# Two attention layers on one core: every attention taken key block by key block, and the side work of the next unit moved behind it

## The chip, the cores and the metric

The kernel runs on one core of a Trainium2 chip. The metric is the device time of one execution in microseconds (us), the median of several. A core has a matrix engine (TensorE, "PE" in the profile; PEld is its weight loads), VectorE (DVE), ScalarE (ACT), GpSimd (POOL) and SyncE (SP), which run their own instruction streams and wait for each other by semaphores.

## The reference

Two layers in sequence on x of 2 images, 32 x 32 pixels, 256 channels (1024 positions an image). Each layer is a group norm, an attention of one head over all positions, and a residual:

```
def layer(x, gamma, beta, wq, bq, wk, bk, wv, bv, wp, bp):      # eps 1e-5, then 1e-6
    xn = group_norm(x, gamma, beta)        # 32 groups of 8 channels, over all positions
    q, k, v = conv1x1(xn, wq, bq), conv1x1(xn, wk, bk), conv1x1(xn, wv, bv)   # B, 1024, 256
    scores = einsum('bnc,bmc->bnm', q, k) / sqrt(256)
    attn = softmax(scores, axis=-1)
    return conv1x1(einsum('bnm,bmc->bnc', attn, v), wp, bp) + x
```

## The kernel before

**Units and chunks.** A unit u is one image in one layer; four units run one after the other (image 0 and 1 in layer 0, then in layer 1). Each has two chunks of 512 queries (c = 2u and 2u + 1), each chunk four query blocks j of 128 and eight key blocks kb of 128. In the loop over units, `before` is the last chunk of the unit before, `first` and `second` are the two of this unit.

**Folded weights.** wq and wk are multiplied once (A), so are wv and wp (Wx). A unit has: t = A by the normalised rows xn (`t_product`, half h = 0 or 1 for the two chunks, two tiles k each), value blocks (`values`, 8), score tiles S (keys by queries, `scores(c, kb)`, 8 a chunk), attention (`attend(c, j, kb)`). Every operand is split into two parts, hi and lo, and each product is three matmuls (hi by lo, lo by hi, hi by hi), to keep the accuracy.

**The path of a score tile.** PE writes it to a PSUM bank; ACT copies it to S (`score_copy`); DVE takes the running maximum into R from the bank (`running_max`), which frees the bank. When all eight are in, PE turns R round (`maxima_by_query`), DVE reduces it (`query_shift`), PE spreads the result over X (`shift_to_all`), DVE adds it to each tile of S (`shifted`), ACT takes the exponential twice (`exponentials`: P_hi, and S in full), POOL subtracts them (`p_low`: P_lo). Then PE can attend. A query block's output is divided by its sum, and added to x in xnat, by DVE (`output`: a reciprocal and a scalar_tensor_tensor), which frees its bank.

**Banks.** Six PSUM banks form a ring. `ring_order` is the list of all tiles (t, V, S, O) in the order in which PE writes them; each waits until the tile six places earlier has been read (`wait_for_bank`). X and Z are the other two banks; Z takes the transposed rows of x and the small products of the group norm.

**The next unit's norm** runs beside this unit's attention: PE transposes pairs of row blocks r = 0 to 3 into Z (`next_rows`), ACT copies them to xraw (`raw_rows`), DVE takes bn_stats (`statistics_of`), after the fourth the aggregate mv (`channel_statistics`), PE multiplies it by group_mean (`mean_of_groups`), DVE forms var_c in four small instructions (`group_deviation`), PE averages it (`variance_of_groups`), DVE and POOL make gain and shift (`variance`, `power`, `affine_map`), then `normalise`, `xn_high`, `xn_low`, and `t_product(u + 1, 0, k)`.

**Order.** Each engine's stream is written out by hand, and each engine does its instructions strictly in that order. PE in a unit: values, scores(first), attention(before), scores(second), attention(first). Before the change the six inner chunks attend query block by query block (all eight key blocks of j = 0, then j = 1, ...), the first and the last chunk key block by key block. The small PE steps stand between query blocks:

```
for j in range(QB):
    ...
    if j == 0: maxima_by_query(following)
    if j == 1: shift_to_all(following); before_third()   # t_product(u, 1, k) in attention(before)
    if j == 2: before_last()                             # next_rows(u+1, 2), or t_product(u+1, 0, k)
```

Of the kernel before, what the change touches and what calls it, by code (L numbers as in the profile page):

```python
# [19 lines left out]
def two_attention_layers(nc, x, layers, vectors, out):  # L20
# [15 lines left out]
    KC = C // P  # L36
    NB = N // P
    HALVES = N // BANK
    CHUNKS = UNITS * HALVES
    QB = BANK // P  # L40
# [26 lines left out]
    for u in range(1, UNITS):  # L67
        ring_order += [("V", u, m) for m in range(NB)]
        ring_order += [("S", 2 * u, kb) for kb in range(NB)]
        ring_order += [("O", 2 * u - 1, j) for j in range(2)]  # L70
        ring_order += [("t", u, 1, k) for k in range(KC)]
        ring_order += [("O", 2 * u - 1, j) for j in range(2, QB)]
        ring_order += [("S", 2 * u + 1, kb) for kb in range(NB)]
        if u < UNITS - 1:
            ring_order += [("O", 2 * u, j) for j in range(3)]
            ring_order += [("t", u + 1, 0, k) for k in range(KC)]
            ring_order += [("O", 2 * u, j) for j in range(3, QB)]
        else:
            ring_order += [("O", 2 * u, j) for j in range(QB)]
    ring_order += [("O", CHUNKS - 1, j) for j in range(QB)]  # L80
    ring_place = {tile: n for n, tile in enumerate(ring_order)}

    with ExitStack() as ctx:
# [66 lines left out]
        Z = ps("Z")  # L150
# [160 lines left out]
        def _(act):  # L311
# [117 lines left out]
            for u in range(1, UNITS):  # L429
# [14 lines left out]

                t_high(u, 1, 0)
                exponentials(first, 0)
                t_high(u, 1, 1)
                exponentials(first, 1)
                exponentials(first, 2)
                if more:  # L450
                    raw_rows(u + 1, 2, Z)
                exponentials(first, 3)

                for kb in range(NB):
                    score_copy(second, kb)
                    if kb == 0 and more:
                        raw_rows(u + 1, 3, Z)
                    if kb in (0, 1, 2, 4):
                        exponentials(first, {0: 4, 1: 5, 2: 6, 4: 7}[kb])

                if more:
                    for q in range(TQ):
                        xn_high(u + 1, q)
                for kb in range(3):
                    exponentials(second, kb)
                if more:
                    for k in range(KC):
                        t_high(u + 1, 0, k)
                exponentials(second, 3)
            for kb in range(4, NB):  # L470
# [4 lines left out]
        def _(dve):  # L475
# [217 lines left out]
            for u in range(1, UNITS):  # L693
# [12 lines left out]

                output(before, 0)
                query_shift(first)
                output(before, 1)
                shifted(first, 0)  # L710
                t_low(u, 1, 0)
                shifted(first, 1)
                t_low(u, 1, 1)
                shifted(first, 2)
                shifted(first, 3)
                output(before, 2)
                shifted(first, 4)
                if more:
                    statistics_of(u + 1, 2)
                shifted(first, 5)  # L720
                output(before, 3)
                shifted(first, 6)

                for kb in range(1, NB):
                    running_max(second, kb)
                    if kb == 1:
                        shifted(first, 7)
                        if more:
                            statistics_of(u + 1, 3)
                            channel_statistics(u + 1)  # L730
                    if more and kb == 5:
                        group_deviation(u + 1)
                    if more and kb == 7:
                        variance(u + 1)
                if more:
                    affine_map(u + 1)

                output(first, 0)
                query_shift(second)
                if more:  # L740
                    normalise(u + 1)
                    xn_low(u + 1, 0)
                    xn_low(u + 1, 1)
                output(first, 1)
                shifted(second, 0)
                shifted(second, 1)
                if more:
                    xn_low(u + 1, 2)
                    xn_low(u + 1, 3)
                output(first, 2)  # L750
                shifted(second, 2)
                if more:
                    t_low(u + 1, 0, 0)
                shifted(second, 3)
                if more:
                    t_low(u + 1, 0, 1)
                output(first, 3)
                shifted(second, 4)
                shifted(second, 5)
# [7 lines left out]
        def _(pe):  # L767
# [191 lines left out]

            def attention(c, following, before_third, before_last):  # L960

                pe.wait_ge(po_P, (c + 1) * NB)
                for j in range(QB):
                    wait_for_bank("O", c, j)
                    for kb in range(NB):
                        attend(c, j, kb)
                    if j == 0:
                        maxima_by_query(following)
                    if j == 1:
                        shift_to_all(following)  # L970
                        before_third()
                    if j == 2:
                        before_last()

            def attention_by_keys(c, kb):
# [23 lines left out]
            for kb in range(NB):  # L999
                scores(1, kb)  # L1000
            for kb in range(NB):
                attention_by_keys(0, kb)
                if kb == 1:
                    maxima_by_query(1)
                if kb == 3:
                    shift_to_all(1)
            for k in range(KC):
                t_product(1, 0, k)

            for u in range(1, UNITS):  # L1010
                before, first, second = 2 * u - 1, 2 * u, 2 * u + 1
                more = u < UNITS - 1

                def second_half():
                    for k in range(KC):
                        t_product(u, 1, k)

                def third_rows():
                    if more:
                        next_rows(u + 1, 2)  # L1020

                def next_first_half():
                    if more:
                        for k in range(KC):
                            t_product(u + 1, 0, k)

                for m in range(NB):
                    values(u, m)

                for kb in range(NB):  # L1030
                    scores(first, kb)
                    if more and kb in (2, 5):
                        next_rows(u + 1, kb // 3)

                attention(before, first, second_half, third_rows)

                for kb in range(NB):
                    scores(second, kb)
                    if kb == 0 and more:
                        next_rows(u + 1, 3)  # L1040
                    if more and kb == 4:
                        mean_of_groups(u + 1)
                    if more and kb == 6:
                        variance_of_groups(u + 1)

                attention(first, second, lambda: None, next_first_half)

            for kb in range(NB):
                attention_by_keys(CHUNKS - 1, kb)

# [31 lines left out]
```

## Time and profile before

| | |
|---|---|
| median of 3 timed runs | 272.69 us (272.2 to 272.89) |
| the profiled execution's own time | 271.55 us |
| its span (first to last instruction) | 269.6 us |
| PE busy | 257.4 us, 95% of the span |
| DVE, ACT, POOL busy | 172.5, 151.1, 110.5 us |
| granted clock of PE, the loop over units | full (1.00) |
| second score stage of unit 1, PE | 109.55 to 122.32 us |

The timeline rows give start and length in us, the engine, the line of the kernel, the operation with its tiles, and in brackets the idle time before it with what ended it. A PE row's length is longer than the distance to the next one, since matmuls overlap; for PE the distances between starts are what counts.

### The profile page before, as it was taken

The page shows a single profiled execution, that of the slowest core. Times are in us where ns is not written, and L with a number is a line of the kernel's source. Part 1 is how long each engine was busy: PE and PEld are TensorE (multiplying, and loading weights), DVE is VectorE, ACT ScalarE, POOL GpSimd, SP SyncE. Part 2 cuts the span into 40 slices and gives each one's busy share as a digit, 9 for nine tenths or more (in the row PEclk, how much of TensorE's full clock was granted, in tenths as well). Part 3 has the DMA queues.
Part 4 walks back from the last instruction along what each step waited for, and adds up shares of the span by engine and source line. Part 5 has one row for each costly group of instructions (what it writes and reads, how often), then busy time and mean ns, then how long its engine had stood idle before and what let it go on. Part 6 is the DMA issues. An engine that isn't in the chain of part 4 may idle for free.

```text
span 269.6 us, 4591 instructions
## 1 busy us (share of the span) xinstructions
PE 257.4 (95%) x1650; PEld 232.8 (86%) x1650; DVE 172.5 (64%) x436; ACT 151.1 (56%) x295; POOL 110.5 (41%) x111
## 2 busy tenths in 40 slices
PE   3899899999999999999999999999999999999994
PEld 2788689889988899879998899879998899889993
DVE  0599576786687557475977557475977547454613
ACT  3465454499778507670687606680577507670750
POOL 2015300187345914451255813461065724550680
PEclk9999999999999999999999999999999999999999
DMA  5960000000000000000000000000110000100102
GB/s 136 368 239 1 0 1 0 2 0 2 0 1 0 4 2 0 0 1 2 0 1 2 0 2 0 0 0 2 40 41 0 4 19 19 39 2 19 58 3 78
DMA packets 5965, 7.37 MB, mean 27 GB/s; under 512 B 556, under 2 KB 4664, under 8 KB 5944
## 3 DMA queue, kind: packets, MB, share of 16 engines
q1 hardware_dynamic: 5920, 7.08, 7.8%
q8 instruction: 13, 0.21, 0.4%
q14 instruction: 8, 0.07, 0.1%
q10 hardware_dynamic: 24, 0.01, 0.0%
HBM read 4.99 MB, written 2.10 MB: 26 GB/s over the span
## 4 chain that ended last, share of the span: by engine, by line
PE 75%; DVE 8%; ACT 8%; issue 6%; DMA 1%; POOL 1%; DVEq 0%; ACTq 0%; POOLq 0%
PE ring L953 10%; PE ring L955 10%; PE ring L954 10%; PE ring L914 9%; PE ring L916 9%; PE ring L915 9%; PE ring L900 3%; PE ring L901 3%; PE ring L902 3%; ACT S L401 2%; PE Z L812 2%; ACT P_hi L400 2%; PE ring L887 2%; PE ring L888 2%; PE ring L889 2%
## 5 line engine op out<-in xcount | busy, mean ns | idle before, releaser
L286 POOL TENSOR_TENSOR P_lo<-S,P_hi 128x512 fp32r<-128x512 f32 x64 | 82.9, 1302 | 104.3 <-ACT S L401 104.3
L953 PE MATMUL ring<-V,P_hi 128*128 128x258 f32 x256 | 73.6, 287 | 0.0
L955 PE MATMUL ring<-V,P_lo 128*128 128x258 f32 x256 | 72.4, 283 | 0.0
L954 PE MATMUL ring<-V,P_hi 128*128 128x256 f32 x256 | 72.3, 282 | 0.0
L393 ACT COPY S<-ring 128x512 f32<-128x512 f32 x64 | 37.6, 587 | 37.4 <-PE ring L916 34.6
L914 PE MATMUL ring<-t_hi,xn_lo 128*128 128x512 f32 x128 | 51.4, 402 | 0.8 <-DVE t_lo L607 0.8
L400 ACT ACTIVATE P_hi<-S 128x512 fp32r<-128x512 f32 x64 | 40.7, 635 | 19.3 <-DVE S L642 17.7
L916 PE MATMUL ring<-t_hi,xn_hi 128*128 128x512 f32 x128 | 50.1, 391 | 0.0
L915 PE MATMUL ring<-t_lo,xn_hi 128*128 128x512 f32 x128 | 49.9, 390 | 0.0
L954 PEld LDWEIGHTS ring<-V,P_hi 128*128 128x128 f32 x256 | 48.5, 189 | 0.5
L953 PEld LDWEIGHTS ring<-V,P_hi 128*128 128x128 f32 x256 | 48.4, 189 | 0.5
L625 DVE TENSOR_TENSOR R<-ring,R 128x512 f32<-128x512 f32 x48 | 33.0, 687 | 24.7 <-ACT S L393 24.1
L955 PEld LDWEIGHTS ring<-V,P_lo 128*128 128x128 f32 x256 | 48.5, 190 | 0.0
L642 DVE TENSOR_TENSOR S<-X,S 128x512 f32<-128x512 f32 x64 | 42.2, 680 | 0.0
L401 ACT ACTIVATE S<-S 128x512 f32<-128x512 f32 x64 | 39.9, 624 | 0.0
L914 PEld LDWEIGHTS ring<-t_hi,xn_lo 128*128 128x128 f32 x128 | 24.1, 188 | 5.5 <-DVE t_lo L607 1.2
L916 PEld LDWEIGHTS ring<-t_hi,xn_hi 128*128 128x128 f32 x128 | 24.0, 188 | 5.2
L915 PEld LDWEIGHTS ring<-t_lo,xn_hi 128*128 128x128 f32 x128 | 24.1, 188 | 4.3
L281 POOL TENSOR_TENSOR xnat<-xnat,out_bias 128x256 f32<-128x256 f32 x32 | 23.0, 754 | 6.3 <-DVE out_bias L517 6.3
L379 ACT ACTIVATE t_hi<-ring,att 128x512 fp32r<-128x512 f32 x16 | 10.6, 681 | 25.0 <-PE ring L889 25.0
L648 DVE RECIPROCAL row_inv<-ring 128x1 f32<-128x1 f32 x32 | 5.2, 164 | 24.0 <-PE ring L955 24.0
L900 PE MATMUL ring<-Wx_hi,xn_lo 128*128 128x258 f32 x64 | 18.5, 290 | 0.2 <-DVE xnat L652 0.2
(100 smaller groups left out, 350.3 us busy)
## 6 DMA issues: line engine op xcount, KB each, us to landing
xnat<-in_x SPq DMA_DIRECT2D x8, 256.0 KB, 6.7
out<-xnat SPq DMA_DIRECT2D x16, 128.0 KB, 1.9
wide<-in_vectors SPq DMA_DIRECT2D x2, 384.0 KB, 6.9
w_wq<-in_L_conv_wq SPq DMA_DIRECT2D x2, 256.0 KB, 4.8
w_wk<-in_L_conv_wk SPq DMA_DIRECT2D x2, 256.0 KB, 4.9
w_wv<-in_L_conv_wv SPq DMA_DIRECT2D x2, 256.0 KB, 6.5
w_wp<-in_L_conv_wp SPq DMA_DIRECT2D x1, 256.0 KB, 6.5
w_wp<-in_L_conv_wo SPq DMA_DIRECT2D x1, 256.0 KB, 6.8
```

The source lines that it names most:

```text
L286: nc.gpsimd.tensor_tensor(P_lo[:, tile, :], S[:, tile, :], P_hi[:, tile, :].bitcast(F32), ALU.subtract).then_inc(po_P, 1)
L393: nc.scalar.copy(S[:, tile_of(c, kb), :], bank_of("S", c, kb)[:]).then_inc(ac_S, 1)
L400: nc.scalar.activation(P_hi[:, tile, :], S[:, tile, :], ACT.Exp)
L401: nc.scalar.activation(S[:, tile, :], S[:, tile, :], ACT.Exp).then_inc(ac_P, 1)
L625: nc.vector.tensor_tensor(R[:], bank_of("S", c, kb)[:], earlier, ALU.max).then_inc(dv_R, 1)
L642: nc.vector.tensor_tensor(tile, X[:], tile, ALU.add).then_inc(dv_D, 1)
L914: nc.tensor.matmul(bank[:], xn_lo[:, kc, keys], t_hi[:, kc, cols], start=(kc == 0), stop=False)
L915: nc.tensor.matmul(bank[:], xn_hi[:, kc, keys], t_lo[:, kc, cols], start=False, stop=False)
L916: last = nc.tensor.matmul(bank[:], xn_hi[:, kc, keys], t_hi[:, kc, cols], start=False, stop=(kc == KC - 1))
L953: nc.tensor.matmul(bank[:, 0:C + 2], P_hi[:, tile, mine], v[:, kb, 0:C + 2], start=(kb == 0), stop=False)
L954: nc.tensor.matmul(bank[:, 0:C], P_hi[:, tile, mine], v[:, kb, C + 2:VX], start=False, stop=False)
L955: last = nc.tensor.matmul(bank[:, 0:C + 2], P_lo[:, tile, mine], v[:, kb, 0:C + 2], start=False, stop=(kb == NB - 1))
```

## The change

1. All eight chunks attend key block by key block: for each kb the four query blocks in turn, so four banks are open until the last kb; a chunk's waits on P_lo are one for each kb. The small steps stand behind key blocks 1 (maxima), 3 (shift) and, in attention(before), 5 (t of this unit's second half).
2. t of the next unit's first half stands behind attention(first), no longer ahead of its last query block; `ring_order` follows.
3. Rows 2 and 3 of the next unit are transposed behind score blocks 1 and 3 of `second` (before: in attention(before), and behind block 0); the mean of the groups is behind block 5 (4), the variance behind block 7 (6).
4. ACT and DVE are rewritten to match: the copies of rows 2 and 3 behind the copies of score blocks 2 and 4, their statistics behind running maxima 3 and 4; t_high behind four exponentials; the four outputs of a chunk together at its end.

```diff
@@ -67,16 +67,12 @@
     for u in range(1, UNITS):
         ring_order += [("V", u, m) for m in range(NB)]
         ring_order += [("S", 2 * u, kb) for kb in range(NB)]
-        ring_order += [("O", 2 * u - 1, j) for j in range(2)]
+        ring_order += [("O", 2 * u - 1, j) for j in range(QB)]
         ring_order += [("t", u, 1, k) for k in range(KC)]
-        ring_order += [("O", 2 * u - 1, j) for j in range(2, QB)]
         ring_order += [("S", 2 * u + 1, kb) for kb in range(NB)]
+        ring_order += [("O", 2 * u, j) for j in range(QB)]
         if u < UNITS - 1:
-            ring_order += [("O", 2 * u, j) for j in range(3)]
             ring_order += [("t", u + 1, 0, k) for k in range(KC)]
-            ring_order += [("O", 2 * u, j) for j in range(3, QB)]
-        else:
-            ring_order += [("O", 2 * u, j) for j in range(QB)]
     ring_order += [("O", CHUNKS - 1, j) for j in range(QB)]
     ring_place = {tile: n for n, tile in enumerate(ring_order)}
@@ -442,31 +438,26 @@
                     if more and kb in (3, 6):
                         raw_rows(u + 1, kb // 3 - 1, Z)
 
-                t_high(u, 1, 0)
-                exponentials(first, 0)
-                t_high(u, 1, 1)
-                exponentials(first, 1)
-                exponentials(first, 2)
-                if more:
-                    raw_rows(u + 1, 2, Z)
-                exponentials(first, 3)
+                for kb in range(4):
+                    exponentials(first, kb)
+                for k in range(KC):
+                    t_high(u, 1, k)
 
                 for kb in range(NB):
                     score_copy(second, kb)
-                    if kb == 0 and more:
-                        raw_rows(u + 1, 3, Z)
-                    if kb in (0, 1, 2, 4):
-                        exponentials(first, {0: 4, 1: 5, 2: 6, 4: 7}[kb])
+                    if kb in (0, 1, 3, 5):
+                        exponentials(first, {0: 4, 1: 5, 3: 6, 5: 7}[kb])
+                    if more and kb in (2, 4):
+                        raw_rows(u + 1, 1 + kb // 2, Z)
 
                 if more:
                     for q in range(TQ):
                         xn_high(u + 1, q)
-                for kb in range(3):
+                for kb in range(4):
                     exponentials(second, kb)
                 if more:
                     for k in range(KC):
                         t_high(u + 1, 0, k)
-                exponentials(second, 3)
             for kb in range(4, NB):
                 exponentials(CHUNKS - 1, kb)
 
@@ -704,58 +695,44 @@
                     if more and kb in (3, 6):
                         statistics_of(u + 1, kb // 3 - 1)
 
-                output(before, 0)
                 query_shift(first)
-                output(before, 1)
-                shifted(first, 0)
-                t_low(u, 1, 0)
-                shifted(first, 1)
-                t_low(u, 1, 1)
-                shifted(first, 2)
-                shifted(first, 3)
-                output(before, 2)
-                shifted(first, 4)
-                if more:
-                    statistics_of(u + 1, 2)
+                for kb in range(5):
+                    shifted(first, kb)
+                for k in range(KC):
+                    t_low(u, 1, k)
+                for j in range(QB):
+                    output(before, j)
                 shifted(first, 5)
-                output(before, 3)
-                shifted(first, 6)
 
                 for kb in range(1, NB):
                     running_max(second, kb)
-                    if kb == 1:
-                        shifted(first, 7)
-                        if more:
-                            statistics_of(u + 1, 3)
-                            channel_statistics(u + 1)
-                    if more and kb == 5:
+                    if kb < 3:
+                        shifted(first, kb + 5)
+                    if more and kb in (3, 4):
+                        statistics_of(u + 1, kb - 1)
+                    if more and kb == 4:
+                        channel_statistics(u + 1)
+                    if more and kb == 6:
                         group_deviation(u + 1)
-                    if more and kb == 7:
-                        variance(u + 1)
                 if more:
+                    variance(u + 1)
                     affine_map(u + 1)
-
-                output(first, 0)
                 query_shift(second)
                 if more:
                     normalise(u + 1)
                     xn_low(u + 1, 0)
                     xn_low(u + 1, 1)
-                output(first, 1)
                 shifted(second, 0)
                 shifted(second, 1)
                 if more:
                     xn_low(u + 1, 2)
                     xn_low(u + 1, 3)
-                output(first, 2)
-                shifted(second, 2)
-                if more:
-                    t_low(u + 1, 0, 0)
-                shifted(second, 3)
-                if more:
-                    t_low(u + 1, 0, 1)
-                output(first, 3)
-                shifted(second, 4)
+                for kb in range(2, 5):
+                    shifted(second, kb)
+                for j in range(QB):
+                    output(first, j)
+                    if more and j in (1, 3):
+                        t_low(u + 1, 0, j // 2)
                 shifted(second, 5)
-            def attention(c, following, before_third, before_last):
-
-                pe.wait_ge(po_P, (c + 1) * NB)
-                for j in range(QB):
-                    wait_for_bank("O", c, j)
-                    for kb in range(NB):
-                        attend(c, j, kb)
-                    if j == 0:
-                        maxima_by_query(following)
-                    if j == 1:
-                        shift_to_all(following)
-                        before_third()
-                    if j == 2:
-                        before_last()
-
...
@@ -998,12 +960,18 @@
                     shift_to_all(0)
             for kb in range(NB):
                 scores(1, kb)
-            for kb in range(NB):
-                attention_by_keys(0, kb)
-                if kb == 1:
-                    maxima_by_query(1)
-                if kb == 3:
-                    shift_to_all(1)
+            def attention(c, behind_sixth):
+
+                for kb in range(NB):
+                    attention_by_keys(c, kb)
+                    if c < CHUNKS - 1 and kb == 1:
+                        maxima_by_query(c + 1)
+                    if c < CHUNKS - 1 and kb == 3:
+                        shift_to_all(c + 1)
+                    if kb == 5:
+                        behind_sixth()
+
+            attention(0, lambda: None)
             for k in range(KC):
                 t_product(1, 0, k)
 
@@ -1014,15 +982,6 @@
                 def second_half():
                     for k in range(KC):
                         t_product(u, 1, k)
-
-                def third_rows():
-                    if more:
-                        next_rows(u + 1, 2)
-
-                def next_first_half():
-                    if more:
-                        for k in range(KC):
-                            t_product(u + 1, 0, k)
 
                 for m in range(NB):
                     values(u, m)
@@ -1032,21 +991,23 @@
                     if more and kb in (2, 5):
                         next_rows(u + 1, kb // 3)
 
-                attention(before, first, second_half, third_rows)
+                attention(before, second_half)
 
                 for kb in range(NB):
                     scores(second, kb)
-                    if kb == 0 and more:
-                        next_rows(u + 1, 3)
-                    if more and kb == 4:
+                    if more and kb in (1, 3):
+                        next_rows(u + 1, 2 + kb // 2)
+                    if more and kb == 5:
                         mean_of_groups(u + 1)
-                    if more and kb == 6:
+                    if more and kb == 7:
                         variance_of_groups(u + 1)
 
-                attention(first, second, lambda: None, next_first_half)
-
-            for kb in range(NB):
-                attention_by_keys(CHUNKS - 1, kb)
+                attention(first, lambda: None)
+                if more:
+                    for k in range(KC):
+                        t_product(u + 1, 0, k)
+
+            attention(CHUNKS - 1, lambda: None)
 
 
 # ---- launch: one core; inputs and outputs as the reference has them ----
```

The three places that matter, as the instruction streams have them. In PE's stream, in the second score stage of unit 1, the mean of the groups (`Z<-mv,group_mean`) before, between score block 4 (ring0) and 5 (ring1):

```order
L916 MATMUL ring0<-t_hi,xn_hi 128x512
L914 MATMUL ring0<-t_hi,xn_lo 128x512
L915 MATMUL ring0<-t_lo,xn_hi 128x512
L916 MATMUL ring0<-t_hi,xn_hi 128x512
L819 MATMUL Z<-mv,group_mean 128x2
L914 MATMUL ring1<-t_hi,xn_lo 128x512
```

And now, between block 5 (ring1) and 6 (ring2):

```order
L893 MATMUL ring1<-t_hi,xn_hi 128x512
L891 MATMUL ring1<-t_hi,xn_lo 128x512
L892 MATMUL ring1<-t_lo,xn_hi 128x512
L893 MATMUL ring1<-t_hi,xn_hi 128x512
L796 MATMUL Z<-mv,group_mean 128x2
L891 MATMUL ring2<-t_hi,xn_lo 128x512
```

It moved back by one score block (the lines' numbers differ since the file is shorter). DVE's stream in the same stage before, from the last two `shifted` to the variance's input (R are running maxima, BN_STATS the statistics of rows 3, BN_AGGR makes mv):

```order
L625 TENSOR_TENSOR R<-ring,S 128x512 [waits ac_S]
L642 TENSOR_TENSOR S<-X,S 128x512 [waits pe_M]
L489 BN_STATS bn<-xraw 128x6 [waits ac_xT]
L489 BN_STATS bn<-xraw 128x6
L523 BN_AGGR mv<-bn 128x2 [waits dv_bn]
L523 BN_AGGR mv<-bn 128x2
L625 TENSOR_TENSOR R<-ring,R 128x512 [waits dv_R,ac_S] x4
L529 COPY gmean<-Z 128x2 [waits pe_gm]
```

And now:

```order
L616 TENSOR_TENSOR R<-ring,R 128x512 [waits dv_R,ac_S]
L480 BN_STATS bn<-xraw 128x6 [waits ac_xT]
L480 BN_STATS bn<-xraw 128x6
L616 TENSOR_TENSOR R<-ring,R 128x512 [waits dv_R,ac_S]
L480 BN_STATS bn<-xraw 128x6 [waits ac_xT]
L480 BN_STATS bn<-xraw 128x6
L514 BN_AGGR mv<-bn 128x2 [waits dv_bn]
L514 BN_AGGR mv<-bn 128x2
L616 TENSOR_TENSOR R<-ring,R 128x512 [waits dv_R,ac_S] x2
L520 COPY gmean<-Z 128x2 [waits pe_gm]
```

The aggregation stood behind the first running maximum of the stage (block 1); it stands behind the fourth (block 4), and two maxima instead of four lie between it and the deviation. ACT's stream in that stage before, from the copy of score block 0 (L393) on; L318 is the copy of rows 3:

```order
L393 COPY S<-ring 128x512 [waits pe_S,po_P]
L318 COPY xraw<-Z 128x2x256 [waits dv_xl,pe_xT]
L400 ACTIVATE P_hi<-S 128x512 [waits dv_D,pe_O]
L401 ACTIVATE S<-S 128x512
L393 COPY S<-ring 128x512 [waits pe_S,po_P]
```

And now, from the copy of block 2 (L389) on; the first L314 is rows 2, the second rows 3:

```order
L389 COPY S<-ring 128x512 [waits pe_S,po_P]
L314 COPY xraw<-Z 128x2x256 [waits dv_xl,pe_xT]
L389 COPY S<-ring 128x512 [waits pe_S,po_P]
L396 ACTIVATE P_hi<-S 128x512 [waits dv_D,pe_O]
L397 ACTIVATE S<-S 128x512
L389 COPY S<-ring 128x512 [waits pe_S,po_P]
L314 COPY xraw<-Z 128x2x256 [waits dv_xl,pe_xT]
```

The copy of rows 3 moved from behind block 0 to behind block 4.

## Rows read from the trace of the kernel before

**Rows 1.** The page: span, busy times, granted clock in 40 slices.
```profile
span 269.6 us, 4591 instructions
...
PE 257.4 (95%) x1650; PEld 232.8 (86%) x1650; DVE 172.5 (64%) x436; ACT 151.1 (56%) x295; POOL 110.5 (41%) x111
...
PEclk9999999999999999999999999999999999999999
```

**Rows 2.** Waits of PE: in total, times, longest; two of the six rows.
```profile
PE Z L823 <- DVE var_c L535: 1.2, 2, 0.6
...
PE ring L900 <- DVE xnat L652: 0.2, 1, 0.2
```

**Rows 3.** Timeline of PE, second score stage of unit 1.
```profile
110.94 0.60 PE L812 MATMUL Z<-ident,xnat 128*128 128x128 f32 x4
111.30 0.48 PE L914 MATMUL ring<-t_hi,xn_lo 128*128 128x512 f32 x1
...
116.86 0.28 PE L819 MATMUL Z<-mv,group_mean 128*128 128x2 f32 x2
...
120.61 0.38 PE L823 MATMUL Z<-var_c,group_mean 128*128 128x2 f32 x2 [0.62 <-DVE var_c L535]
```

**Rows 4.** Timeline of ACT, the same stage.
```profile
111.20 0.59 ACT L393 COPY S<-ring 128x512 f32<-128x512 f32 x1 [2.57 <-PE ring L916]
111.68 0.59 ACT L318 COPY xraw<-Z 128x512 f32<-128x512 f32 x1
...
113.21 0.58 ACT L393 COPY S<-ring 128x512 f32<-128x512 f32 x1
```

**Rows 5.** Timeline of DVE, the same stage.
```profile
113.83 0.69 DVE L625 TENSOR_TENSOR R<-ring,S 128x512 f32<-128x512 f32 x1 [2.72 <-ACT S L393]
114.44 0.68 DVE L642 TENSOR_TENSOR S<-X,S 128x512 f32<-128x512 f32 x1
115.03 0.74 DVE L489 BATCH_NORM_STATS2 bn<-xraw 128x6 f32<-128x256 f32 x2
115.81 0.39 DVE L523 BATCH_NORM_AGGREGATE mv<-bn 128x2 f32<-128x24 f32 x2
...
119.34 0.69 DVE L625 TENSOR_TENSOR R<-ring,R 128x512 f32<-128x512 f32 x1 [0.92 <-ACT S L393]
...
120.39 0.16 DVE L535 TENSOR_TENSOR var_c<-dev,mv 128x2 f32<-128x2 f32 x1
```

**Rows 6.** Timeline of PE, attention by keys (60), by queries (215); 24 matmuls between.
```profile
60.60 0.29 PE L953 MATMUL ring<-V,P_hi 128*128 128x258 f32 x1
...
63.51 0.60 PE L940 MATMUL X<-ident,R 128*128 128x128 f32 x4
...
215.43 0.29 PE L953 MATMUL ring<-V,P_hi 128*128 128x258 f32 x1
...
218.31 0.60 PE L940 MATMUL X<-ident,R 128*128 128x128 f32 x4
```

**Rows 7.** Timeline of PE and DVE, end of a query block and its output.
```profile
96.84 0.60 PE L940 MATMUL X<-ident,R 128*128 128x128 f32 x4
...
97.31 0.48 DVE L652 SCALAR_TENSOR_TENSOR xnat<-ring,row_inv,xnat 128x256 f32<-128x256 f32 x1
```

**Rows 8.** Timeline of PE, ACT and DVE, from unit 0 to unit 1.
```profile
74.39 0.39 PE L887 MATMUL ring<-xn_hi,A_lo 128*128 128x512 f32 x1
...
77.56 0.39 PE L900 MATMUL ring<-Wx_hi,xn_lo 128*128 128x258 f32 x1 [0.16 <-DVE xnat L652]
...
75.39 1.30 ACT L379 ACTIVATE t_hi<-ring,att 128x512 fp32r<-128x512 f32 x2
...
76.08 0.75 DVE L607 SCALAR_TENSOR_TENSOR t_lo<-ring,att,t_hi 128x512 fp32r<-128x512 f32 x1 [0.89 <-ACT t_hi L379]
...
77.02 0.48 DVE L652 SCALAR_TENSOR_TENSOR xnat<-ring,row_inv,xnat 128x256 f32<-128x256 f32 x1
...
77.68 0.48 DVE L652 SCALAR_TENSOR_TENSOR xnat<-ring,row_inv,xnat 128x256 f32<-128x256 f32 x1
```

## The prediction, made before the changed kernel was run

> **What bounds the kernel now.** I read the page first: TensorE (PE) is busy 95% of a span of 269.6 us, at the full granted clock in nearly every slice [rows 1]. Then the waits of PE: inside the loop over units it waits for the variance of the groups, twice, 1.2 us in all, and once 0.2 us for an output row [rows 2]; the list's other four rows name two transfers, t_lo and neg_shift, and stand in unit 0 or ahead of it. So from the first unit on the time is the number of matmuls times their pace. A change of order can win about those waits and no more; each new wait of PE is added in full, since nothing later has slack to give it back. The question is therefore which of PE's semaphores will come after PE gets there.
>
> All times below are starts of PE instructions ("PE reaches"), because a PE row's length overlaps the next row. By that measure one key block of scores costs 1.36 us: rows of x end at 111.30 and the mean of the groups is reached at 116.86, that is 5.56 us for four key blocks, of which 0.11 us is the first matmul behind a transposition (0.34 us to its follower against 0.23 us) [rows 3].
>
> **The change part by part.**
>
> *Key block by key block.* Every matmul stays. The weights of each matmul change as they did, the outputs go over four banks in turn, and each key block has a wait of its own on P_lo instead of one wait for all eight. The first and the last chunk run so already: 24 matmuls of attention took 2.91 us there (60.60 to 63.51) and 2.88 us query by query (215.43 to 218.31) [rows 6]. The difference is 0.03 us in 24, at most 0.7 us for the six chunks that change; two rows that close don't separate it from nothing, so the sum takes 0 and the range 0.7. Could it gain? Only if PE waited for P_lo at the start of a chunk; none of the six rows of PE's waits is for P_lo [rows 2], so the looser wait gives nothing. The Trainium skill, "TensorE: Matmul & The Clock Gate", section "A second HAM failure mode: psum-queue depth-cycling", speaks against such an order: cycling through PSUM banks made short idle times between groups of matmuls, and the clock fell again and again. By the row the order costs 0, by the page it could cost much; the trace of this case doesn't agree with it.
>
> *Rows 2 and 3 of x and their statistics, two tiles later.* This is the term that decides. Before, rows 2 were transposed inside the attention and rows 3 behind score block 0 of the second chunk, and PE asked for the mean of the groups behind block 4. The aggregates were ready at 115.81 + 0.39 = 116.20 us [rows 5], PE came at 116.86 [rows 3]: 0.66 us to spare. Now rows 2 stand behind block 1, rows 3 behind block 3, ScalarE (ACT) copies rows 3 only behind its copy of score block 4, and VectorE (DVE) takes their statistics behind the running maximum of block 4. PE asks for the mean behind block 5. The chain, from the moment PE ends block 4:
> - ACT starts copying the block 0.26 us later (110.94 to 111.20) [rows 3, 4].
> - DVE starts the running maximum 0.62 us after the copy starts (113.21 to 113.83), and the next instruction 0.61 us later [rows 4, 5]. That is 1.49 us. The copy of rows 3 ends at 0.26 + 0.48 + 0.59 = 1.33 us [rows 4], so it isn't last.
> - Two bn_stats and the gap to the aggregation 0.78 us, the aggregation 0.39 us [rows 5], the semaphore 0.06 us (var_c ends at 120.55, PE goes on at 120.61) [rows 3, 5].
> The sum is 2.72 us. PE has one block of 1.36 us in that time and then stands: **1.36 us of a new wait**, for the mean, in each of the two units that have a successor: +2.7 us. Nothing before it on ACT is late: two exponentials take 1.05 us (111.68 + 0.48 to 113.21) [rows 4], so block 3 with its exponentials ends 0.26 + 0.48 + 1.05 = 1.79 us after PE's end of block 3, and block 4's copy isn't due before 1.36 + 0.45 (transpositions and refill, rows 3) + 0.26 = 2.07 us. Queued behind the waiting matmul are the score blocks 6 and 7; the whole PE stream moves.
>
> *The variance wait.* Before: behind block 6, waiting for var_c, which came at 120.55 after a running maximum started at 119.34, 1.21 us [rows 5]. PE's idle time there is 0.62 us by the row [rows 3]; from start to start it is 0.26 + 0.62 + 1.21 + 0.06 - 1.36 = 0.79 us, and the difference is the tail of the last matmul. After: behind block 7, var_c behind the maximum of block 6: the same lag of one block, so the same 0.79 us. The exponentials that now stand before that copy end 1.79 us after block 5, and the new wait gives them time. This term is 0: the old wait stays and the new one comes on top.
>
> *Outputs at the end of an attention, four at once.* Behind attention(before), three times, score block 0 of the second chunk needs the bank of that attention's first output. PE ends a query block's last matmul, and the output row is written 0.95 us later (96.84 to 97.31 + 0.48) [rows 7]; the first of four queries ends 9 matmuls of 0.12 us, 1.09 us, before PE is through. So the bank is free 0.14 us before it is wanted, less 0.06 us for the semaphore. I take no stall, but a lost early load of weights, the 0.11 us of a refill, three times: +0.3 us. The next outputs follow at 0.66 us (77.02 to 77.68) [rows 8] and the score blocks at 1.36 us. DVE must be free: t_lo of the second half now comes just before. PE's t ends 24 matmuls, 2.9 us, ahead of the end; 0.26 us and t_hi of 0.65 us and t_lo of 0.75 us [rows 8] end at 1.2 us ahead. The first output's reciprocal is due 0.27 us before its row of 97.31, that is 0.2 us behind its last matmul and 0.9 us ahead of the end: 0.3 us of slack for DVE. Thin, but there. If it is missed by as much as one t_lo, 0.75 us, three times, that is +2.2 us: the upper end of this term.
>
> *t of the next unit behind the attention.* Unit 1 has this order already, and pays for it: value block 2 waits 0.16 us for its bank, held by an output that queued behind t_lo on DVE [rows 8]. There ACT came to t_hi late (75.39, when PE's first t tile had ended at 74.39) because of exponentials. In the changed units the fourth exponential ends, by the same lengths, over a microsecond before t_hi is due, so t_lo starts 0.26 + 0.69 us behind the first t tile (six matmuls at 0.23 us, 1.4 us), 2.35 us after the attention; the third output row is written at 2.35 + 0.94 + 0.48 = 3.8 us [rows 8], and the bank is wanted behind both t tiles and two value blocks of six matmuls at 0.12 us, at 2.8 + 2 x 0.72 = 4.2 us. I take 0; the bound is the row of unit 1, 0.4 us from start to start, twice: 0.8 us.
>
> *Sum.* 2.7 + 0 + 0 + 0.3 + 0 = +3.0 us. The profiled execution took 271.55 us around its span, so 274.6 us; it lies 1.1 us below the median of the timed runs, 272.69, from which the same sum gives **275.7 us**, 1.1% slower.
>
> **Rivals.**
> - *The mean's wait doesn't come.* For it: it is reckoned, not seen. Against: for that the statistics would have to land 1.36 us sooner, and every link above is a row of this kernel. Then only the 0.3 us is left: 273.0 us, no change that can be told (a measurement of this kernel tells about 0.3%, 0.8 us). 0.11.
> - *More waits than one.* DVE is late with the first output, or value blocks wait as in unit 1: 2.2 + 0.8 us at the outside, about half of it likely if at all: 277.2 us. For it: the slack is 0.1 to 0.3 us. 0.13.
> - *Faster.* The variance wait goes because DVE, freed of outputs in that stretch, has var_c 0.79 us sooner, and the mean isn't late. Both would win 2 x 0.79: 271.1 us. It decides at var_c 0.79 us after block 6's maximum instead of 1.21 us behind it, which four dependent instructions don't allow. 0.05.
> - *The clock falls.* In the trace it held through PE's idle 0.62 us [rows 1, 3]; the new idle is 1.2 us by the same measure, which no row inside the loop shows. If PE ran at 1.2 GHz for the rest of that stage, two score blocks, 2.7 us more per unit: 281 us. The Trainium skill, "TensorE: Matmul & The Clock Gate", section "HAM oscillation — how this bites in real kernels", has the clock fall in idle gaps; its example waits longer than this. 0.02. That it falls through the order by keys itself, every 24 matmuls then taking 2.9 us more, 24 times, +70 us, has [rows 6] against it: under 0.01.
>
> **How the numbers follow.** The forecast has 0.68. Its own range is 274.7 to 276.7. The whole range, 273.2 to 277.8 us, takes in half of the first rival's ground and most of the second. Faster by over 0.3% is the third rival, 0.05; within 0.3% is the first with a little of the forecast's low side, 0.13; slower 0.82.
>
> **What the changed profile would show.** Among PE's waits a new row: group_mean for DVE's mv (the aggregation), two times, 1.1 to 1.3 us each by the row's idle time; the variance row still two times 0.6 us. The second score stage of units 1 and 2 longer by 1.4 us, unit 3 as long as before. 24 matmuls of attention in 2.9 us. Score block 0 of the second chunk with a small wait or none for xnat. The prediction is wrong if PE lists no wait for mv, or if a wait for xnat or t_lo stands above it.

## The result and the profile after

The changed kernel takes 275.15 us (median of 4 runs, 274.87 to 275.88), the kernel before 272.44 us (4 runs, 271.52 to 272.89): ratio 1.0108, 95% interval 1.0073 to 1.0142. That is 1.1% slower, 2.7 us, against a forecast of 275.7 us, +3.0.

The waits of PE in the changed kernel (in total, times, longest) answer to [rows 2]:

```profile
PE Z L796 <- DVE mv L514: 2.5, 2, 1.2
...
PE Z L800 <- DVE var_c L526: 1.5, 2, 0.9
...
PE ring L877 <- DVE xnat L643: 0.2, 1, 0.2
```

The first row is new: PE waits at the mean of the groups (L796) for the aggregation of the statistics, once in each of the two units that have a successor. The variance row, 1.2 us before, is still there and grew by 0.3 us. No row names P_lo. The xnat row is that of unit 1's start, as before.

Busy time by unit, before and then after (stretches from the first value block of units 1, 2 and 3; the last ends with PE's last matmul; behind the length stand the busy times of PE, PEld, DVE, ACT and POOL, then the granted clock):

```profile
75.79:137.52 61.73, 60.95 (x397) 55.24 (x396) 41.68 (x103) 34.93 (x68) 27.12 (x26) 1.00 0.01 1
137.52:198.73 61.21, 60.59 (x399) 55.15 (x397) 41.11 (x102) 34.94 (x68) 26.96 (x26) 1.00 0.03 8
198.73:265.63 66.90, 66.90 (x462) 62.33 (x460) 36.68 (x83) 34.78 (x68) 32.74 (x30) 1.00 0.06 18
```

```profile
76.42:140.12 63.70, 61.41 (x398) 55.08 (x396) 42.12 (x103) 35.80 (x69) 28.38 (x27) 1.00 0.00 1
140.12:203.09 62.97, 61.13 (x397) 54.98 (x396) 41.17 (x102) 35.53 (x68) 26.77 (x25) 1.00 0.02 5
203.09:270.08 66.99, 66.99 (x461) 62.40 (x459) 35.82 (x83) 34.60 (x67) 31.07 (x28) 1.00 0.06 20
```

The first number behind the stretch is its length. Units 1 and 2 are 1.97 and 1.76 us longer, unit 3 by 0.09 us: 3.82 us in this pair of profiles, nearly all of it where side work for a next unit exists. The clock is full in all six stretches. The interval of the ratio is 2.0 to 3.9 us, so the profiles' 3.82 us lie at its upper end.

Where the two measures differ, the setup is part of it: unit 1 starts at 75.79 before and at 76.42 after, and in the profiles of the changed kernel's variants below, whose code up to there is the same, anywhere from 75.27 to 76.49. The units repeat more closely: one of these variants (e8) changes nothing but waits for P_lo, on which PE doesn't stand in units 1 and 2, and has them within 0.03 us of the changed kernel's. So the sums below use the units' lengths; but each is from one profiled execution, and the timed runs are given beside them.

### The profile page after: what moved, and what is told of

It is laid out like the page before. It is cut to its first block, busy times and chain, and to the rows that moved or that the text cites. A ratio compares the mean times of both kernels' runs of the same rounds, so it can differ in the third digit from the quotient of the medians.

```text
span 274.1 us, 4591 instructions
## 1 busy us (share of the span) xinstructions
PE 259.1 (95%) x1650; PEld 233.0 (85%) x1650; DVE 172.2 (63%) x436; ACT 152.4 (56%) x295; POOL 109.9 (40%) x111
## 4 chain that ended last, share of the span: by engine, by line
PE 75%; DVE 9%; ACT 7%; issue 6%; DMA 1%; POOL 1%; DVEq 0%; ACTq 0%; POOLq 0%
PE ring L930 10%; PE ring L932 10%; PE ring L931 10%; PE ring L891 9%; PE ring L893 9%; PE ring L892 9%; PE ring L877 3%; PE ring L878 2%; PE ring L879 2%; ACT S L397 2%; ACT S L389 2%; PE Z L789 2%; PE ring L865 2%; PE ring L864 2%; PE ring L866 2%
## 5 line engine op out<-in xcount | busy, mean ns | idle before, releaser
L389 ACT COPY S<-ring 128x512 f32<-128x512 f32 x64 | 37.5, 586 | 41.1 <-PE ring L893 37.0
L633 DVE TENSOR_TENSOR S<-X,S 128x512 f32<-128x512 f32 x64 | 41.4, 682 | 8.6 <-PE X L923 8.6
L598 DVE SCALAR_TENSOR_TENSOR t_lo<-ring,att,t_hi 128x512 fp32r<-128x512 f32 x16 | 11.6, 746 | 11.5 <-ACT t_hi L375 11.5
L878 PE MATMUL ring<-Wx_lo,xn_hi 128*128 128x258 f32 x64 | 18.2, 284 | 0.0
```

Source lines behind the costliest of these rows:

```text
L389: nc.scalar.copy(S[:, tile_of(c, kb), :], bank_of("S", c, kb)[:]).then_inc(ac_S, 1)
L633: nc.vector.tensor_tensor(tile, X[:], tile, ALU.add).then_inc(dv_D, 1)
```

## The chain behind the new wait, row by row

The changed kernel's timelines of PE, ACT and DVE, unit 1, second score stage; score block 4 ends at 117.73, where block 5's first matmul starts:

```profile
117.73 0.40 PE L891 MATMUL ring<-t_hi,xn_lo 128*128 128x512 f32 x1
...
118.88 0.39 PE L893 MATMUL ring<-t_hi,xn_hi 128*128 128x512 f32 x1
120.52 0.35 PE L796 MATMUL Z<-mv,group_mean 128*128 128x2 f32 x2 [1.25 <-DVE mv L514]
...
124.62 0.38 PE L800 MATMUL Z<-var_c,group_mean 128*128 128x2 f32 x2 [0.88 <-DVE var_c L526]
...
117.98 0.59 ACT L389 COPY S<-ring 128x512 f32<-128x512 f32 x1 [0.26 <-PE ring L893]
118.46 0.59 ACT L314 COPY xraw<-Z 128x512 f32<-128x512 f32 x1
...
118.60 0.69 DVE L616 TENSOR_TENSOR R<-ring,R 128x512 f32<-128x512 f32 x1 [0.55 <-ACT S L389]
119.21 0.74 DVE L480 BATCH_NORM_STATS2 bn<-xraw 128x6 f32<-128x256 f32 x2
119.98 0.39 DVE L514 BATCH_NORM_AGGREGATE mv<-bn 128x2 f32<-128x24 f32 x2
```

From PE's end of block 4 the copy starts 0.25 us later, the maximum 0.62 us behind it, the statistics 0.61 us behind that, the aggregation 0.77 us on, and ends at 120.37; PE goes on at 120.52. That is 2.79 us, reckoned 2.72: from the aggregation's end to PE it took 0.15 us, not 0.06. The last matmul of block 5 starts at 118.88, and its follower could have at 119.11, so PE stood 1.41 us from start to start, 1.25 us by the row. Reckoned: 1.36.

## Experiments

"Loop" is the length of units 1 to 3 in the profile, as above: 189.84 us before, 193.66 us after. Each ratio is to runs of the kernel before that were taken beside the experiment: 23 of them with median 272.12 us for e1 to e4, 19 with median 271.71 us for e5 to e8.

**The mean one block later** (label e1_mean_later):

```diff
-                    if more and kb == 5:
+                    if more and kb == 6:
                         mean_of_groups(u + 1)
```

> The changed kernel with one number altered: PE asks for the mean of the groups behind score block 6 instead of 5. Theory (the whole loss is PE waiting for the aggregation of the statistics, 1.4 us in each of two units): the aggregation lands 2.8 us after block 4 ends, PE now comes 2.7 us after it, so the wait for mv shrinks to 0 to 0.1 us, the wait for var_c stays at 0.6 to 0.9 us, and the time falls by 2.6 to 2.8 us, to the time of the kernel before or 0.3 us above it. Rival (order by keys or bunched outputs cost): it stays 1 us or more above the kernel before.

Measured: 272.50 us, ratio to the kernel before 1.0004 (0.9982 to 1.0026); loop 190.37 us. PE's waits no longer name mv, and for var_c, where the expectation had 0.6 to 0.9 us each, are down to

```profile
PE Z L800 <- DVE var_c L526: 0.9, 2, 0.5
```

One number gives back 3.29 us of the loop's 3.82: 2.8 us are the two waits, 0.5 us more is saved at the variance, where the mean's own two matmuls and the refill behind them (0.22 + 0.11 us) now stand between block 6 and PE's arrival. The order by keys with everything else of the change is left 0.53 us above the kernel before in the loop, and can't be told from it by the timed runs. That isn't yet the price of the rest, since the wait for var_c is 0.3 us shorter here than in the kernel before; e6 and e7 compare the two orders with neither wait.

**The mean one block earlier** (e2_mean_earlier; the same edit with 4):

> The changed kernel with PE asking for the mean behind score block 4 instead of 5. Theory: PE's wait for mv grows by the one score block it no longer has, 1.36 us a unit, to 2.6 us of idle time by the row, and the time by 2.7 us, to about 278 us. Rival (other instructions behind the wait absorb it): less than 1.5 us more.

Measured: 280.79 us, 5.6 us above the changed kernel where 2.7 was expected, ratio 1.0318 (1.0266 to 1.0371). The four timed runs spread from 279.04 us, with a mean granted clock of 0.993, to 282.78 us, with 0.982. The profiled execution is the slowest of them: its loop is 200.6 us, 6.9 us above the changed kernel's. The wait grew as the theory says, from 1.25 to 2.63 us by the row. Most of the rest is the clock. Timeline of PE in unit 2, and the stretches around the two waits (length, busy times, then the granted clock):

```profile
183.45 0.40 PE L893 MATMUL ring<-t_hi,xn_hi 128*128 128x512 f32 x1
186.47 0.56 PE L796 MATMUL Z<-mv,group_mean 128*128 128x2 f32 x2 [2.63 <-DVE mv L514]
186.89 0.78 PE L891 MATMUL ring<-t_hi,xn_lo 128*128 128x512 f32 x1
187.46 0.63 PE L892 MATMUL ring<-t_lo,xn_hi 128*128 128x512 f32 x1
187.89 0.63 PE L893 MATMUL ring<-t_hi,xn_hi 128*128 128x512 f32 x1
```

```profile
116.05:120.31 4.26, 1.64 (x10) 1.06 (x8) 3.45 (x9) 2.53 (x5) 1.27 (x1) 1.00 0.00 0
120.31:127.61 7.30, 6.42 (x23) 4.87 (x23) 2.13 (x7) 2.80 (x5) 1.28 (x1) 0.77 0.00 1
182.21:186.47 4.26, 1.63 (x9) 1.06 (x8) 3.45 (x9) 2.53 (x5) 1.26 (x1) 0.96 0.00 0
186.47:194.58 8.11, 7.86 (x22) 6.00 (x23) 1.84 (x6) 2.62 (x5) 1.28 (x1) 0.60 0.00 0
```

Behind the wait matmuls start 0.43 us apart instead of 0.23, the lower level of 1.2 GHz: at once in unit 2, and 1.0 us behind the wait's end in unit 1. The granted clock is 0.77 and 0.60 on average until the score stage ends. So the theory's dose holds for the wait, and the expectation missed its consequence.

**Rows 2 and 3 one block earlier, mean where the change has it** (e3_rows_earlier):

```diff
-                    if more and kb in (1, 3):
+                    if more and kb in (0, 2):
                         next_rows(u + 1, 2 + kb // 2)
...
+                    if more and kb in (0, 2):
+                        raw_rows(u + 1, 2 + kb // 2, Z)
                     if kb in (0, 1, 3, 5):
                         exponentials(first, {0: 4, 1: 5, 3: 6, 5: 7}[kb])
-                    if more and kb in (2, 4):
-                        raw_rows(u + 1, 1 + kb // 2, Z)
...
-                    if more and kb in (3, 4):
-                        statistics_of(u + 1, kb - 1)
-                    if more and kb == 4:
+                    if more and kb in (2, 3):
+                        statistics_of(u + 1, kb)
+                    if more and kb == 3:
                         channel_statistics(u + 1)
```

> The changed kernel with rows 2 and 3 one score block earlier on PE (behind 0 and 2), their copies on ACT ahead of the exponentials there, their statistics behind running maxima 2 and 3, the mean still behind block 5. Theory: the aggregation lands about 1.36 us sooner, as PE reaches it; 2.5 to 2.8 us less than the changed kernel, the same as moving the mean. Rival (the place of the mean in PE's stream matters, not the data's arrival): no gain.

Measured: 273.58 us, ratio 1.0053 (1.003 to 1.0075), 1.6 us less than the changed kernel; loop 191.48 us, 2.2 us less. Its wait for mv:

```profile
PE Z L796 <- DVE mv L514: 0.5, 2, 0.3
```

So it is the arrival of the data, not the mean's place in PE's stream. The gain is short of the 2.5 to 2.8 us expected, by 0.3 us in the loop and 0.9 us in the timed runs. A third of a microsecond of the wait is left in each unit, and the timelines of unit 1 say where: ACT copies score block 2 0.60 us behind PE's end of it, not 0.26, since it comes out of two exponentials; DVE, which has a shift and the statistics of rows 2 behind that maximum, starts block 3's 1.00 us behind its copy, not 0.62.

**The side work moved alone, attention query by query** (e4_rows_alone): the kernel before with these edits on PE, and with the copies, exponentials and statistics of that stage on ACT and DVE as the change has them:

```diff
-                attention(before, first, second_half, third_rows)
+                attention(before, first, second_half, lambda: None)
...
-                    if kb == 0 and more:
-                        next_rows(u + 1, 3)
-                    if more and kb == 4:
+                    if more and kb in (1, 3):
+                        next_rows(u + 1, 2 + kb // 2)
+                    if more and kb == 5:
                         mean_of_groups(u + 1)
-                    if more and kb == 6:
+                    if more and kb == 7:
                         variance_of_groups(u + 1)
```

> The kernel before, attention query by query as it was, with only the side work moved as in the change: rows 2 and 3 behind score blocks 1 and 3, copies and statistics with them, mean behind 5, variance behind 7. Theory: this alone costs what the change costs, a wait for mv of 1.2 us in two units, 2.7 us in all, 275.2 us. Rival (order by keys costs a good part): clearly less, under 1.5 us above the kernel before.

Measured: 275.79 us, ratio 1.0127 (1.0088 to 1.0165); loop 193.89 us, 4.05 us above the kernel before. Units 1 and 2 are 1.88 and 1.56 us longer than before, against 1.97 and 1.76 us in the changed kernel: nearly the whole loss, without a change of the attention:

```profile
PE Z L816 <- DVE mv L521: 2.5, 2, 1.2
PE Z L820 <- DVE var_c L533: 1.5, 2, 0.9
...
PE ring L950 <- POOL P_lo L286: 0.4, 1, 0.4
```

It also has a wait that the change doesn't: P_lo, 0.4 us, in unit 3. It makes unit 3 0.6 us longer. The exponentials of the last key blocks come later in the new stage, and the query order needs all eight P_lo at once.

**One wait for all eight P_lo in the order by keys** (e8_wait_for_all):

```diff
-                pe.wait_ge(po_P, c * NB + kb + 1)
+                if c in (0, CHUNKS - 1):
+                    pe.wait_ge(po_P, c * NB + kb + 1)
+                elif kb == 0:
+                    pe.wait_ge(po_P, (c + 1) * NB)
```

> The changed kernel with one wait for all eight P_lo at the start of each inner chunk, as the query order had, instead of one for each key block. It asks what the looser wait is worth. Theory: the exponentials of the last four key blocks now end up to 1.1 us later than before, so the last unit, whose PE isn't held by the mean, would wait 0.4 to 0.6 us for P_lo once; the other chunks not at all: 0.5 us more than the changed kernel. Rival: the waits for each key block have a cost of their own, and the time falls.

Measured: 276.04 us, ratio 1.0155 (1.0113 to 1.0197); unit 3 is 67.61 us against 66.99, the others within 0.03 us. The wait is the one of the run before:

```profile
PE ring L930 <- POOL P_lo L282: 0.4, 1, 0.4
```

What the order by keys buys is this: cover for late exponentials, 0.6 us once, and only because the change made them late. The seven waits a chunk more cost nothing that units 1 and 2 show.

**The variance behind the first key block of the attention** (e5_variance_behind), the changed kernel with

```diff
-                    if more and kb == 7:
-                        variance_of_groups(u + 1)
-                attention(first, lambda: None)
+                attention(first, lambda: None, (lambda: variance_of_groups(u + 1)) if more else None)
...
                     attention_by_keys(c, kb)
+                    if kb == 0 and behind_first:
+                        behind_first()
```

> The changed kernel with the variance of the groups behind the first key block of attention(first) instead of behind score block 7; the mean stays behind block 5. Theory: PE comes 1.45 us later, after var_c, so that wait (0.6 to 0.9 us of idle time, 0.75 to 1.0 us from start to start, twice) goes and the wait for mv stays at 1.2 us: 1.7 us less than the changed kernel, about 1.0 us above the kernel before. Rival (the affine map, now 1.2 us later on DVE, delays the shift or xn_lo and PE waits there): no gain, with a wait for neg_shift or xn_lo in its place.

Measured: 273.82 us, ratio 1.0075 (1.0048 to 1.0103), 1.3 us less than the changed kernel; loop 191.60 us, 2.06 us less, 1.7 expected. PE lists mv twice, 2.5 us in all as before the edit, and var_c not at all, and no wait for xn_lo.

**Both moved** (e6_both_moved: this edit and the mean behind block 6):

> The changed kernel with both moved: the mean behind score block 6, the variance behind the first key block of attention(first). Theory: neither wait is left and the two units end 2.1 us sooner each than in the changed kernel; 0.9 to 1.4 us below the run with the mean alone moved, 1 us below the kernel before (ratio 0.996). Rival: the side work comes too late for the next t, PE waits for xn_lo, no gain over the kernel before.

Measured: 270.74 us, ratio 0.9965 (0.9942 to 0.9988); loop 188.87 us, 1.50 us below the run with the mean alone moved. None of PE's waits lies in units 1 to 3 but the xnat row of unit 1's start.

**The kernel before with the variance moved** (e7_before_variance):

```diff
                     for kb in range(NB):
                         attend(c, j, kb)
+                        if j == 0 and kb == 3 and within_first:
+                            within_first()
...
-                    if more and kb == 6:
-                        variance_of_groups(u + 1)
...
-                    if more and kb == 7:
-                        variance(u + 1)
                 if more:
+                    variance(u + 1)
                     affine_map(u + 1)
...
-                attention(first, second, lambda: None, next_first_half)
+                attention(first, second, lambda: None, next_first_half,
+                          (lambda: variance_of_groups(u + 1)) if more else None)
```

> The kernel before, query block by query block, with one step moved: the variance inside the first query block of attention(first), behind its fourth key block, DVE's part behind all running maxima. Theory: its wait for var_c, 0.8 us from start to start, twice, goes: 1.5 us less than the kernel before (ratio 0.994). Rival: in this order t of the next unit stands ahead of the last query block, 2.9 us earlier than in the changed kernel, and xn_lo is late for it; then half or all of the gain is lost in a wait for xn_lo.

Measured: 270.02 us, ratio 0.993 (0.9906 to 0.9955), the fastest; loop 187.99 us, 0.9 us below the changed order with both moved (0.7 us by the timed medians). Neither kernel waits for mv or var_c, so this is what the change costs apart from the two waits: 0.34, 0.45 and 0.09 us in units 1, 2 and 3. DVE and PE in unit 1 show how little room the query order has:

```profile
128.36 1.29 DVE L571 TENSOR_TENSOR xn_lo<-xraw,xn_hi 128x512 fp32r<-128x512 f32 x2
...
130.68 0.39 PE L886 MATMUL ring<-xn_hi,A_lo 128*128 128x512 f32 x1
```

xn_lo's first half ends at 129.65, and PE takes up t, which waits for it, at 130.68: 1.0 us to spare.

## Why the prediction was right

- **The new wait for the mean**, reckoned at 1.36 us twice, measured 1.41 us from start to start in unit 1. It was right, and shown three ways: it goes with the mean one block later (e1), with the data earlier (e3), and comes with the side work alone (e4).
- **The variance wait**, reckoned unchanged at 0.79 us. In unit 2 it was; in unit 1 it grew, by the row from 0.62 to 0.88 us. ACT's copy of score block 6 starts 0.53 us behind PE's end of the block there instead of 0.26. It does so in the kernel before too, where it cost nothing, since var_c hung on block 5, and in unit 1 of nearly every experiment. A packet of the instruction queue starts 0.65 us behind that copy in both profiles; whether ACT was waiting for its own instructions wasn't tried, and the cause stays open. Moving var_c's source to block 6 exposed the delay. The term was mis-sized by 0.27 us.
- **The order by keys**, taken at 0 with a bound of 0.7 us: unit 3, which has it in two more chunks and no side work, is 0.09 us longer, no more than the outputs' term below, so hardly anything is left for the order of the matmuls. 24 matmuls of attention take 2.86 to 2.99 us in either kernel. The looser wait on P_lo, taken as worth nothing, is worth 0.6 us in unit 3 (e8), since the change itself makes the exponentials late. The falling clock, which the prediction weighed for such an order, didn't come: 1.00 in all stretches.
- **Outputs at once**, 0.11 us three times for a lost early load of weights: score block 0's first matmul is 0.47 us long and the next one starts 0.31 us behind it, 0.08 us more than the usual 0.23, and its start 0.03 us late. Its weights are loaded at 109.77, 0.03 us ahead of it, where the kernel before has 0.11 us. Together 0.11 us, as reckoned, though by another path: the prediction has the whole 0.11 us in the distance to the follower, by a row behind a transposition that it reads as 0.34 us and that is 0.32 (111.30 to 111.62):

```profile
109.80 0.47 PE L891 MATMUL ring<-t_hi,xn_lo 128*128 128x512 f32 x1
110.11 0.39 PE L892 MATMUL ring<-t_lo,xn_hi 128*128 128x512 f32 x1
```

- **t behind the attention**: 0 reckoned, and no wait for xnat in units 2 and 3.
- **The score stage**: the prediction has it 1.4 us longer in units 1 and 2. It is 2.29 and 2.07 us longer, because the transposition of rows 2 now stands in it; the attention that had it is 0.4 us shorter. This moves time between stages and leaves the sum as it is.
- **The sum** was 3.0 us; the timed runs give 2.7, the loop 3.8. The loop has 2.8 us for the mean, 0.3 for the first unit's variance and 0.3 for the outputs. Of the 0.4 us left, 0.3 are gaps under 0.1 us that the prediction has no term for, 0.08 us at the second transposition and 0.07 at the mean's own two matmuls, in both units. So the sum is 0.8 us short of the loop; the timed runs, whose interval holds both numbers, can't show it.
- **What the order by keys asks for**: rows 2 of the images of units 2 and 3 are outputs of the chunk `before`, query blocks 0 and 1. Query by query they are ready in the middle of that attention; key block by key block all four outputs come at its end. So the rows had to move behind it. This is read from the code. That they stand behind score blocks 1 and 3, with the mean behind 5, is a choice: e3 has the rows one block earlier and e1 the mean one block later, and both give most of the loss back.
- **The rivals**: that PE wouldn't wait is refuted, and so is the faster one: by itself the change takes no wait away. Of "more waits than one" nothing came: PE has no new wait for an output or for t_lo, only the variance wait that grew. The clock fell in none of the changed kernel's stretches, but it is a real rival one block further on (e2).

## What to carry to other kernels

When one engine runs without gaps, a small step that it must take for another engine's benefit (here a matmul of two columns) costs what its input is late, in full, and more where the clock falls behind the wait. Place such a step by counting from its input: the start of the chain's first link, each link's length from a row, and the number of the busy engine's blocks in that time. Here moving the step by one block gave back 3.3 us of the loop, moving its input's source 2.2 us, and the variance's place (1.9 us in the kernel before) was worth more than the order of the whole attention.

## What was not expected of the hardware

A wait of PE of 1.25 us by the row left the clock at 1.00, in both units and likewise in e4, e5 and e8. One of 2.63 us, one block earlier, was followed by matmuls at half pace (0.43 us instead of 0.23 from start to start) and a granted clock of 0.77 and 0.60 over the next 7.3 and 8.1 us. In the profiled execution, the slowest of four, the second step of 1.36 us so cost 3.5 us a unit, by the timed medians 2.8 us, where the first cost 1.4. The Trainium skill, "TensorE: Matmul & The Clock Gate", section "HAM oscillation — how this bites in real kernels", tells of this with waits on transfers; here the clock fell behind a wait for VectorE.
